# Four edge passes of a graph network kernel: the row gathers wait once per chunk of four steps in place of once per step

## What is computed

```python
x = _layernorm(x + _L0_gnn_ref(x, ...))   # two GATv2 layers: softmax over a target's edges
x = _layernorm(x + _L1_gnn_ref(x, ...))   # sums over the source nodes
x = _layernorm(x + _L2_gnn_ref(x, ...))   # one attention layer, then a GRU cell
x = _layernorm(x + _L3_gnn_ref(x, ...))   # eight heads of attention
```

```python
xj = xl[src]                                  # a row of 128 floats for each edge
logits = leaky_relu(xj + xr[dst]) @ att       # layer 2: score_dst[dst] + score_src[src]
ex = exp(logits - segment_max(logits)[dst])
out = segment_sum(ex * xj) / segment_sum(ex)
```

## Time and profile before

| what | value |
|---|---|
| median of three runs | 14911.71 us |
| the profiled execution's own time | 14998.32 us |
| its span, first to last instruction | 14996.4 us |
| TensorE busy | 11026.0 us (74%) |
| GpSimd busy | 9489.8 us (63%) |
| VectorE busy | 7973.5 us (53%) |
| ScalarE busy | 5541.4 us (37%) |
| mean granted TensorE clock | 0.72 |

### The profile page before, as it was taken

How to read it: one execution, slowest core, us unless ns; L and a number is a source line. 1 busy time by engine, 2 the same in 40 slices (tenths; PEclk the granted TensorE clock), 3 DMA queues, 4 the chain that set the end, 5 groups by cost and what they waited for, 6 DMA issues and landing times.

```text
span 14996.4 us, 278163 instructions
## 1 busy us (share of the span) xinstructions
PE 11026.0 (74%) x60653; PEld 8678.6 (58%) x60653; DVE 7973.5 (53%) x29240; ACT 5541.4 (37%) x14105; POOL 9489.8 (63%) x8593
## 2 busy tenths in 40 slices
PE   5777777777777778888888875555555767777776
PEld 4666666666666666666666653344344556666664
DVE  6555555555555555555555553333333566666666
ACT  1444444344444444333333343333333622222223
POOL 3666666466666657888888865566666255655555
PEclk7887788788778775766666765555555877888777
DMA  3111111221111113444444452222222221222222
GB/s 87 45 45 44 44 45 45 88 80 44 45 44 45 44 40 44 39 39 39 39 39 39 39 104 58 44 45 45 45 45 45 60 52 48 50 49 49 50 50 56
DMA packets 808955, 748.01 MB, mean 50 GB/s; under 512 B 264685, under 2 KB 691174, under 8 KB 808254
## 3 DMA queue, kind: packets, MB, share of 16 engines
q0 software_dynamic: 453440, 550.05, 21.1%
q1 hardware_dynamic: 354814, 191.38, 4.9%
HBM read 548.62 MB, written 192.13 MB: 49 GB/s over the span
## 4 chain that ended last, share of the span: by engine, by line
PE 27%; another core or an unknown queue 15%; issue 13%; DMA 9%; DVE 7%; ACT 6%; POOL 2%; SPq 1%; DVEq 1%; ACTq 0%; POOLq 0%
DMA scatter_s<-dst_side 8%; PE bank L738 8%; PE bank L721 3%; PE bank L722 3%; PE bank L1214 3%; ACT oh_e L826 2%; PE bank L1220 2%; PE bank L1229 2%; PE bank L747 2%; PE bank L705 1%; POOL scatter_s L1181 1%; DVE agg L960 1%; DVE lrelu L915 1%; DVE agg L951 1%
## 5 line engine op out<-in xcount | busy, mean ns | idle before, releaser
L738 PE MATMUL bank<-rows,oh_e 128*128 128x130 f32 x9984 | 2172.6, 376 | 1578.7 <-ACT oh_e L826 1172.1
L1181 POOL DMA_INDIRECT scatter_s<-dst_side x1664 | 2568.6, 1544 | 551.9 <-DMA scatter_s<-dst_side 267.1
L738 PEld LDWEIGHTS bank<-rows,oh_e 128*128 128x128 f32 x9984 | 1804.0, 264 | 1918.7 <-issue 1036.4
L826 ACT ACTIVATE oh_e<-bank,weight,minus_w 128x128 f32<-128x128 f32 x4992 | 1880.3, 459 | 2378.4 <-remote 1620.8
L951 DVE SCALAR_TENSOR_TENSOR agg<-agg,rescale,bank 128x130 f32 x4992 | 1683.4, 337 | 1636.6 <-remote 792.6
L722 PE MATMUL bank<-rows,ident 128*128 128x128 f32 x9984 | 2335.9, 319 | 144.8 <-issue 141.1
L687 POOL DMA_INDIRECT rows<-gather_c,edge_sb x1664 | 1650.9, 992 | 1122.4 <-issue 443.9
L687 POOL DMA_INDIRECT rows<-gather_b,edge_sb x1664 | 1672.5, 1005 | 1061.9 <-issue 423.0
L687 POOL DMA_INDIRECT rows<-gather_a,edge_sb x1664 | 1669.1, 1003 | 1008.5 <-issue 412.0
L687 POOL DMA_INDIRECT rows<-gather_s,edge_sb x1664 | 1574.3, 946 | 1061.2 <-issue 443.2
L722 PEld LDWEIGHTS bank<-rows,ident 128*128 128x128 f32 x9984 | 1894.7, 235 | 159.7 <-issue 157.6
(11 more groups left out here) (352 smaller groups left out, 18169.2 us busy)
## 6 DMA issues: line engine op xcount, KB each, us to landing
rows<-gather_a,edge_sb POOLq DMA_INDIRECT x1664
rows<-gather_b,edge_sb POOLq DMA_INDIRECT x1664
scatter_s<-dst_side POOLq DMA_INDIRECT x1664
rows<-gather_s,edge_sb POOLq DMA_INDIRECT x1664
rows<-gather_c,edge_sb POOLq DMA_INDIRECT x1664
rows<-scatter_s SPq DMA_DIRECT2D x56, 455.0 KB, 6.3
scatter_s<-zeros SPq DMA_DIRECT2D x64, 390.0 KB
edge_sb<-edge_tab SPq DMA_DIRECT2D x520, 40.0 KB
```

Of the source, the lines that this page charges most:

```text
L738: ins = e.matmul(sum_bank(g)[:, (g % 2) * AW:(g % 2) * AW + L.aw], oh_e[:, g % 8, :], r, start=True, stop=True)
L826: e.activation(oh_e[:, g % 8, :], bank[7][:, (g % CH) * P:(g % CH + 1) * P], ACT.Relu, bias=weight[:, it.slot(2, 2), g:g + 1], scale=minus ...
L1181: e.indirect_dma_start(scatter_s[k], bass.IndirectOffsetOnAxis(ap=S_.target[:, it.slot(1), g:g + 1], axis=0), S_.summed[:, g % 8, :], None ...
```

## The change

The constant `LEAD` goes. An edge pass gets a number `behind`: 2 in the vector passes, 1 in the third pass. Before the four gathers of chunk c, GpSimd waits once, for the last step (the fourth) of the target sides of chunk c - `behind`, counted through the group boundary. The four gathers are then issued with no wait between them. The wait for `L.block` stays. Nothing is changed on the other engines.

```diff
-LEAD = 10
...
+                self.behind = 2 if vector else 1
...
                 for c in range(NCH):
                     w.hold_ge(L.block.at(it, c, lag=U))
+                    used = (c - L.behind) * CH + CH - 1
+                    w.hold_ge(L.side.at(it, used) if c >= L.behind else L.side.at(it, used + G, lag=1))
                     for g in range(c * CH, (c + 1) * CH):
-                        w.hold_ge(L.side.at(it, g - LEAD) if g >= LEAD else L.side.at(it, g + G - LEAD, lag=1))
                         e.indirect_dma_start(rows[:, u, g, 0:L.width], None, L.src_rows,
                                              bass.IndirectOffsetOnAxis(ap=edge_sb[:, u, g:g + 1].bitcast(I32), axis=0)
                                              ).then_inc(L.gat[c].sem(it), 16)
```

## The result

The changed kernel takes 14982.77 us (median of seven runs, 14953.41 to 15013.82), the kernel before on the same chip 14907.03 us (seven runs, 14893.13 to 14938.14). The ratio is 1.0049, with a 95% interval of 1.0037 to 1.0060: **slower by 0.5%**, 76 us. The forecast was 14770 us and faster, with 0.38 for slower. The likelier side was the wrong one; the time lies within the range.

The account below looks back on a forecast made before the run. The prediction took a loop of gathers and late-reported sides to bound all four edge passes. Waits and later gathers counted 0, stops -145 us: 14998 to 14853, less 87 for the profiled execution, about 14770 us; range 14350 to 15300.

Parts of the forecast that it names:

- What bounds the kernel: All four edge passes: GpSimd waits for sides, reported late while gathers run; 5 us of gathers, then a 1.6 us stop.
- Twelve waits a group gone, 0: GpSimd: 16 waits for sides a group become 4, done while the gather before still runs, so 0 us.
- The gathers start later in the vector passes, 0: Vector passes: gathers held two to five steps longer, yet rows land before TensorE needs them, so costed at 0.
- The cover of 3.5 us: Vector passes: a chunk's last gather lands after 7.1 us, its sides start after 10.6 us, leaving 3.5 us.
- The upper bound, 312 us: Vector passes: where late reports nearly use up the cover, at most one microsecond a group, 312 us in three passes.
- Third pass one chunk back, 0: Third pass: gathers wait nine to six steps later, but VectorE needs rows only at the turn's end; cover 6.5 us, 0.
- -52 forecast for E2: Third pass: stops fall from 3.2 to 2.9 a group, idle time in stops from 535 to 483 us.
- The stops, -145: GpSimd, all edge passes: fewer stops a group at 1.6 us, longer in the last; -28 -28 -52 -37 us.
- The execution that the sum was read from: Whole kernel: the profiled execution, 86.6 us above the median, so 87 us was subtracted from 14853 us.
- Lockstep: Rival, all edge passes: sides reported only after each run of four gathers; 26.4 us a group, 15202 up to 15516 us; 0.38.
- Opening the loop by fewer waits: Rival, edge passes: late reports come from GpSimd's own waits, so fewer waits halve the stops; 13880 us; chance 0.12.
- No change: Rival, edge passes: stops only move, as many and as long; 14912 us; chance 0.10 together with the fourth rival.

Follow-up runs that it names:

- free_b: All GpSimd waits for sides deleted, only the wait for block sums kept, on a chip where the kernel before takes 14986 us; ratio 1.2189.
- third_only: The chunk's wait in the third pass alone, old waits in the vector passes; ratio 1.0007 to the kernel before at 12870 us.
- free: All GpSimd waits for sides deleted, only the wait for block sums kept, where the kernel before takes 12870 us; ratio 1.0002.
- after_c: The changed kernel as it stands, on a chip where the kernel before takes 14924 us; ratio 1.0044.
- four_waits: The changed kernel with the chunk's wait repeated before each of its four gathers; ratio 1.0244 to the kernel before at 12870 us.
- vec_only: The chunk's wait in the vector passes alone, old waits in the third pass; ratio 1.0243 to the kernel before at 12870 us.
- E1: Not a run: the second of the kernel's four edge passes, a vector pass; 2632 us in the first profile of the kernel before.
- lead7: The kernel before with a lead of 7 steps in place of 10 in the vector passes alone; ratio 1.0014 to 14972 us.
- third_only_b: The chunk's wait in the third pass alone, old waits elsewhere, on a chip where the kernel before takes 14986 us; ratio 0.9979.
- vec_only_b: The chunk's wait in the vector passes alone, on a chip where the kernel before takes 14986 us; ratio 1.0123.
- behind3: The changed kernel waiting one chunk further back in every pass (three, in the third pass two); ratio 1.0001 to the kernel before at 14899 us.
- lead13: The kernel before with a lead of 13 steps in place of 10 in the vector passes alone; ratio 1.0240 to 14972 us.
- before_again: The kernel before, unchanged, profiled again on the chip where it takes 14899 us.
- after_again: The changed kernel, unchanged, profiled on the chip where the kernel before takes 14899 us; ratio 1.0042.

## Why the prediction was wrong

**What bounds the kernel: right, and confirmed.** Where the kernel before takes 14900 us, gathers and late reports set the pace of the passes. free_b shows it from one side, and the chip with 12870 us from the other: without stops E0 takes 2131 us in third_only, within 3% of 1664 x 1.25. S1, which has no such waits, is the same on both kinds of chip (3082 us from first to last scatter in free, 3079 in after_c).

**Twelve waits a group gone, 0: right.** four_waits and vec_only differ by 0.0001.

**The gathers start later in the vector passes, 0: wrong, and this is the step that turned the sign.** The cover of 3.5 us was worked out from one window with a landing of 2.8 us and a release seen at once, and it was asked only whether TensorE would wait for rows, not whether GpSimd would wait for the release. vec_only shows that second wait by itself, where no report is late: 273 stops and 254 us where there were next to none. In the changed kernel TensorE waits 400.1 us for landings over the three passes where 70.8 stood before, 259.9 of them in E3; the test that the prediction had set (under 100 us a pass) fails in E3 and holds in E0 (49.8) and E1 (90.4). The upper bound, 312 us, would have held the cost on the slower chips: +0.69% of 14924 is 103 us on one and +1.23% of 14986 is 184 on another; +2.43% of 12870 is 313. I named the bound and took zero in the sum. How the loss divides between GpSimd's waits, TensorE's and the longer gathers on the slower chips stays open: lead7 has as much waiting for landings (374.0 us) and costs 0.14%.

**Third pass one chunk back, 0: right.** third_only on the 12870 us chip: 1.0007, no stop in E2. Where reports are late it gains: 0.9979, or 31 us, in third_only_b. There the stops gave part of the -52 forecast for E2 (508 us in stops in its E2, 526 in vec_only_b's).

**The stops, -145: wrong by its size.** The count went as forecast: 331 to 284 in E0 is 3.2 to 2.7 a group, and in E2 3.7 to 2.5. (The 2.8 of the forecast was idle time divided by 1.6 and not a count; the trace has 324 stops in E0, 3.1 a group, of 1.40 us beyond 0.30.) Runs are of four and eight, but for 18 stops of E0's 280 in the changed kernel, which stand behind the first gather of a chunk, 0.9 us each. But I had taken one price for a stop, 1.6 us, before and after. It grew with the run before it, in E0 from 1.27 to 1.50 us beyond the usual 0.30, in E2 from 1.36 to 2.03. A wait for the last of four sides ends later than a wait for one of them. The idle time in stops stayed what it was or grew: 421 to 425 us in E0, 438 to 422 in E1, 525 to 519 in E2, 540 to 597 in E3. The likely gain of -145 became +39 in this pair of profiles (in the first pair, whose profile before was the long one, -55). The forecast's own sign for E2, idle time near 1000 us, did not come: 1036.8 without the opening wait, and 1033.7 in the earlier trace rows.

**The execution that the sum was read from: not the ordinary one.** The profiled execution of the kernel before lay 87 us above the median, and I took that as an offset on top of the passes. It was in the very stops that I was counting: the earlier trace rows have 1008.5 us of idle time in E0, the second profile of the same kernel 975.3. The forecast's own test came true for E0, 932 us without the opening wait against 983.1 - 48.2 = 934.9; but the kernel before, in its ordinary execution, has 975.3 - 48 = 927 already. What I read as a gain of 28 us was one execution's difference from the next.

**The rivals.** Lockstep gave the right sign with the wrong mechanism: the stops did not go to 3.5 a group. Opening the loop by fewer waits is refuted, since four_waits and free on one chip and free_b on another show no gain from waits left out. No change came nearest in size, 14912 against 14983. The page's rule, "DMA: Bandwidth & Descriptors" of the Trainium skill, section "Rules for kernel authors", to issue a DMA early and wait for it late, had the right sign for this change: holding gathers back lost in the vector passes on all five chips (on one of them by lead7's 0.14% alone), and behind3 won it back on the chip where it ran. It does not hold without limit here: issuing three steps earlier than the kernel before (lead13) loses 2.4%, and as early as the slots allow (free_b) 22%, on chips where the reports are late.

No kernel that ran on both kinds of chip beats the kernel before on both. third_only, the chunk wait in the third pass alone, comes nearest: 0.9979 (0.9969 to 0.9988) where the kernel before takes 14986 us, and 1.0007 with no change told where it takes 12870.

## What to carry to other kernels

When a wait is moved to a coarser unit, ask for each instruction behind it which event it waits for now and then, in units of what the other engine produces: here the first gather went from the third side of the chunk three back to the last side of the chunk two back, and in the vector passes the chunk's wait cost 0.7% to 2.4%. Don't multiply a new count of stalls by the old length of a stall: here, where two engines hold each other up, the idle time per round stayed the same in E0 and E2. And profile the kernel before twice, on more than one chip if they can be had, before reading differences of half a per cent from it.

## What the runs showed that was not expected

- **One kernel, two speeds by chip.** The kernel before takes 12870 us on one chip and 14899 to 14986 on four others, 16% more. S1 is the same on both; the edge passes differ, 2078 against 2605 us for E2 at the same granted clock of 0.50.
- **On the slower chips a run of gathers holds back the reports between engines.** Over the 194 runs of eight in behind3's E0, TensorE's increments arrive at some 0.1 per half us late in a run, and from 1.2 to 1.8 us after the run has ended at 5 to 8 per half us. With runs of sixteen, TensorE and ScalarE stand still for 7 us. The waiting engines start as late as the increments arrive. What differs between the chips, and what holds an increment back, the runs don't show.
- **The best distance depends on the chip.** Where reports are late, a lead of 7 steps costs 0.14% against 10, a chunk wait with leads of 9 to 12 nothing, 13 costs 2.4% and no limit 22%. Where they are in time, 10 steps and no limit are equal (1.0002), and the leads between were not run.
- **Gathers of the vector passes are sometimes long, and the long ones meet a multiply of VectorE.** They take up to 1.9 us where the median is 0.95; in the third pass none takes over 1.13. Each of the 504 long ones (over 1.1 us) in E0 and E1 of the changed kernel overlaps the multiply by the attention vector (L916 there, L915 before), and so do all 322 of before_again; nearly all end 0.8 us after it, whenever they began. The third pass has no such multiply. Two pairs from the changed kernel's E0:

```profile
1487.18 0.67 DVE L916 TENSOR_TENSOR lrelu<-lrelu,att 128x512 f32<-128x512 f32 x1
1487.35 1.32 POOL L688 DMA_INDIRECT rows<-gather_a,edge_sb  x1 [0.30 <-issue]
...
1492.81 0.67 DVE L916 TENSOR_TENSOR lrelu<-lrelu,att 128x512 f32<-128x512 f32 x1
1492.93 1.37 POOL L688 DMA_INDIRECT rows<-gather_a,edge_sb  x1 [0.30 <-issue]
```

  The gathers end at 1488.67 and 1494.30, 0.82 us after the multiplies' ends at 1487.85 and 1493.48. The page "SBUF — State Buffer" of the Trainium skill, section "SBUF: two separate sides", says that a VectorE instruction with two SBUF inputs and a GpSimd instruction that reads SBUF hold a shared pair of ports in turn, each for its whole instruction. The trace agrees: the multiply reads `lrelu` and `att`, and the gather its indices from `edge_sb`. With the chunk's wait more gathers meet a multiply, 168 to 247 in E0 and 154 to 263 in E1 (before_again to after_again). They are 20 and 43 us of the loss on that chip (busy 1667.3 to 1687.5 and 1656.0 to 1699.0), and 5 and 20 between third_only_b and vec_only_b. No run took the multiply away.
